# Gate and up products moved into the steps of attention, down and output projection into one last stage

## The reference

```
xn = layernorm(x)
# attention: 32 query heads, 8 key/value heads of width 32, causal, rotary positions
q, k, v = rope(xn @ wq), rope(xn @ wk), xn @ wv
s = softmax(mask(q @ k.T / sqrt(32))) @ v  @ wo
# feed-forward: 2,752 hidden features, weights packed in 4 bits with scales and zeros per group
W    = scale[group] * (nibble - (zero[group] + 1))
g    = silu( (silu(xn @ W_gate) * (xn @ W_up)) @ W_down )
out  = x + s * g
```

## Time and profile before

| | |
|---|---|
| median of three executions | 2513.79 us (2512.66 to 2514.32) |
| the profiled execution | 2516.59 us |
| its span, first to last instruction | 2514.5 us |
| mean granted clock of TensorE | 0.973 of 2.4 GHz |
| instructions | 46,178 |
| TensorE busy | 2377.0 us, 95% |
| VectorE busy | 1545.8 us, 61% |
| ScalarE busy | 748.2 us, 30% |
| GpSimd busy | 942.3 us, 37% |

### The profile page before, as it was taken

One profiled execution on the slowest core, in us unless ns is written; L12 is line 12 of the kernel. 1 busy time (PEld: TensorE's weight loads), 2 busy tenths in 40 slices (PEclk: granted clock), 3 DMA queues, 4 the chain that ended last, 5 costly groups with the idle time before them and its releaser, 6 DMA issues.

```text
span 2514.5 us, 46178 instructions
## 1 busy us (share of the span) xinstructions
PE 2377.0 (95%) x17048; PEld 1229.9 (49%) x17048; DVE 1545.8 (61%) x2800; ACT 748.2 (30%) x1469; POOL 942.3 (37%) x619
## 2 busy tenths in 40 slices
PE   6999889999999699989999999999999999999998
PEld 3555356666666444434444444444444444444432
DVE  4655488888888577355555555646454555556465
ACT  3222157777777532211111111010101010202022
POOL 2555469999999600021121212121212120202035
PEclk9999979999999899999999999999999999999998
DMA  5332312221222264200000000000000000000056
GB/s 159 97 84 64 86 43 72 72 71 59 70 72 72 89 198 163 82 16 13 12 13 13 12 12 12 5 19 3 21 0 24 0 24 0 24 0 19 0 172 234
DMA packets 129662, 138.26 MB, mean 55 GB/s; under 512 B 33106, under 2 KB 106421, under 8 KB 129148
## 3 DMA queue, kind: packets, MB, share of 16 engines
q1 hardware_dynamic: 127228, 127.96, 16.8%
q10 hardware_dynamic: 2304, 8.39, 0.8%
HBM read 88.76 MB, written 47.42 MB: 54 GB/s over the span
## 4 chain that ended last, share of the span: by engine, by line
PE 53%; DVE 3%; issue 1%; ACT 0%; POOL 0%; DVEq 0%; POOLq 0%
PE dn_ps L1474 18%; PE gate_ps L1455 17%; PE up_ps L1455 16%; PE s_ps L1424 1%; DVE zero L1542 1%; DVE wf L1554 0%; DVE dif L1548 0%; PE s_ps L1432 0%; ACT arena L1636 0%; PE z_ps L1424 0%; DVE acc L1586 0%; DVE nib L1523 0%; DVE zhalf L1537 0%; DVE idf L1502 0%; DVE acc L1579 0%
## 5 line engine op out<-in xcount | busy, mean ns | idle before, releaser
L1455 PE MATMUL gate_ps<-xT,wg 128*128 128x512 f16 x2112 | 789.1, 381 | 3.8 <-POOL wg L1676 3.8
L1455 PE MATMUL up_ps<-xT,wg 128*128 128x512 f16 x2016 | 766.1, 380 | 0.0
L577 POOL TENSOR_TENSOR p_lo<-probs 128x1152 f16<-128x1152 f32 (+1 forms) x256 | 501.2, 1994 | 48.8 <-ACT probs L741 48.7
L1474 PE MATMUL dn_ps<-wd,hT 128*128 128x512 f16 (+1 forms) x2112 | 471.9, 383 | 3.1 <-DVE acc L1579 3.1
L1676 POOL TENSOR_TENSOR wg<-wf,wg 128x512 f16<-128x512 f32 (+1 forms) x88 | 99.8, 1134 | 869.9 <-ACT wg L1622 869.9
L741 ACT ACTIVATE probs<-sc_ps 128x512 f32<-128x512 f32 (+3 forms) x768 | 351.0, 490 | 123.7 <-PE sc_ps L685 105.1
L1474 PEld LDWEIGHTS dn_ps<-wd,hT 128*128 128x128 f16 (+1 forms) x2112 | 202.2, 98 | 270.2 <-issue 31.5
L1579 DVE TENSOR_TENSOR acc<-acc,dn_ps 128x512 f32<-128x512 f32 x320 | 219.8, 687 | 184.7 <-PE dn_ps L1474 184.5
L1455 PEld LDWEIGHTS gate_ps<-xT,wg 128*128 128x128 f16 x2112 | 208.5, 99 | 242.0 <-issue 9.8
L790 DVE TENSOR_REDUCE shift<-mx_wide_ps 128x1 f16<-128x1024 f32 (+3 forms) x256 | 262.0, 1023 | 84.6 <-PE mx_wide_ps L667 84.5
L1455 PEld LDWEIGHTS up_ps<-xT,wg 128*128 128x128 f16 x2016 | 197.6, 98 | 229.9 <-issue 2.4
(11 more groups left out here) (130 smaller groups left out, 2973.7 us busy)
## 6 DMA issues: line engine op xcount, KB each, us to landing
o_scratch<-o SPq DMA_DIRECT2D x16, 1040.0 KB, 4.9
a<-o_scratch SPq DMA_DIRECT2D x16, 1040.0 KB, 5.4
arena<-q_scratch SPq DMA_DIRECT2D x48, 256.0 KB, 3.4
arena<-in_qw_d SPq DMA_DIRECT2D x42, 256.0 KB
xin<-in_x SPq DMA_DIRECT2D x16, 512.0 KB, 3.7
s_scratch<-arena ACTq DMA_DIRECT2D x16, 512.0 KB, 2.6
xT<-in_x SPq DMA_DIRECT2D x32, 256.0 KB, 4.8
xT<-s_scratch SPq DMA_DIRECT2D x32, 256.0 KB, 5.6
```

Of the source, the lines that this page charges most:

```text
L577: eng.tensor_tensor(p_lo[:, r % 2, c], probs[:, r % 2, c], p_hi[:, r % 2, c], ALU.subtract).then_inc(done, 1)
L1455: last = pe.matmul(to[q][:, :], wg[:, u, wp, s, g * P:(g + 1) * P], xT[:, xp, s, t * BANK:(t + 1) * BANK], start=(s == 0 and k == 0), stop ...
L1474: last = pe.matmul(dn_ps[n][:, :], hT[0:w, hp, e, tokens], wd[0:w, wp, e, n * BANK:(n + 1) * BANK], start=(e == 0 and p == 0), stop=(e == ...
```

## The change

`attend` and the gate and up part of `feed_forward` become one block, `attend_and_expand`. Its step is one head together with one unit, that is one tile of hidden features by one chunk of 512 tokens; there are 64 heads and 88 units, so 64 joint steps are followed by 24 with a unit alone, and ahead of them stand four lead-in steps with maxima and the first tile's weights. In each of the 8 slots of a step stand 6 gate or up products. Hidden values go to DRAM (`ht_d`), and so do the rebuilt down weights (`wd_d`).

Weights are rebuilt in half rounds of 256 columns, 12 to a tile. Zeros are no longer packed: their table is as wide as the scales' and is spread by a product with only the first 8 (down: 21) rows of the selection. VectorE doesn't unpack zeros any more.

Maxima use the high parts alone, 32 rows a head, and two heads go side by side: the loads place the high part of even heads in rows 0 to 31 and of odd heads in rows 32 to 63. The shifts are turned by VectorE. GpSimd forms all low parts of the probabilities.

The tables are built in `project_qkv`, 10 pieces over 20 of its blocks, and `xin` has 3 buffers there.

`finish` holds the output projection and the down projection: each tile of 128 tokens reads its hidden values from DRAM; down weights of all 22 tiles lie in the place of `xT` and elsewhere, and the sum over the 22 tiles stays in PSUM.

```diff
 def load_heads(eng, q_d, k_d, qT, kT, qk_loaded, g, u):
-    for piece, (qp, kp) in enumerate([(0, 0), (0, 1), (1, 0)]):
+    for piece, (qps, kp) in enumerate([((0, 1), 0), ((1, 0), 0), ((0,), 1)]):
...
# project_qkv
-    XB = 4
+    XB = 3
...
+            def tables_at(e):
+                c = (e - CT - 1) // 2
+                if 0 <= c < NP:
+                    piece(c, (e - CT - 1) % 2)
+                if e == CT + 2 * (NP + 1) + 2:
+                    select()
...
                 if e >= 1:
                     join(e - 1)
+                tables_at(e)
...
+def half_rounds(t):
+    halves = [(1, "g", 2 * t), (5, "g", 2 * t + 1)]
+    if t >= 2:
+        halves += [(3, "d", 2 * t - 4), (7, "d", 2 * t - 3)]
+    return sorted(halves)
...
# attend_and_expand
-    SC_BANKS = 3
+    SC_BANKS = 2
+    LEAD = 6
+    MAXIMA = [(7, 0), (7, 1), (0, 0), (6, 0), (6, 1), (1, 0), (5, 0), (2, 0), (5, 1), (4, 0), (3, 0), (4, 1)]
...
+            def maxima(m, r, k):
+                u, q, n = r // REP, r % REP, NM * pair(m, r) + k
+                t, c = MAXIMA[k]
...
+                if not isinstance(m, int) or n >= 1:
+                    pe.wait_ge(mx_taken, n)
+                first, end = c * BANK, min((c + 1) * BANK, (t + 1) * P)
+                diagonal = end == (t + 1) * P
+                for e in range(2):
+                    rows = slice(e * HD, (e + 1) * HD)
+                    last = pe.matmul(mx_ps[:, e, 0:end - first], qT[rows, u, q + e, t * P:(t + 1) * P],
+                                     kT[rows, u, first:end], start=True, stop=not diagonal)
+                if diagonal:
+                    for e in range(2):
+                        last = pe.matmul(mx_ps[:, e, t * P - first:end - first], identb[:, :], maskb[:, :],
+                                         start=False, stop=True)
+                last.then_inc(mx_ready, 1)
...
+            def rebuild(kind, n, j, u, number):
...
+                    rows = sel_gu[:, :].rearrange("g (p s) -> g s p", s=KT)[:, n, :]
+                    pe.matmul(sz_ps[:, 0, 0:2 * w], rows, st[:, u, :, 0:w], start=True, stop=True)
+                    last = pe.matmul(sz_ps[:, 1, 0:2 * w], rows[0:G_GU, :], zt[:, u, :, 0:w], start=True, stop=True)
+                else:
...
+                    pe.matmul(sz_ps[0:w, 0, :], sel[:, u, 0:w], scd[:, cols], start=True, stop=True)
+                    last = pe.matmul(sz_ps[0:w, 1, :], sel[0:G_D, u, 0:w], zd[:, cols], start=True, stop=True)
...
+            def step(m, r):              # TensorE
+                for i in range(ST):
+                    scores(m, r, i)
+                    for slot, kind, n, j, u, number, _ in halves(m, r):
+                        if slot == i:
+                            rebuild(kind, n, j, u, number)
+                    if maxima_at(m, r, i):
+                        maxima(*maxima_at(m, r, i))
+                    if i == 1:
+                        outputs(*at(m, r, -1, R), 0)
+                    if i >= 1:
+                        outputs(*at(m, r, -1, R), i)
+                    gate_up(m, r, i)
...
+            def step(m, r):              # ScalarE
+                for i in range(ST):
+                    exps(m, r, i)
+                    if i == 0:
+                        copy_sums(*at(m, r, -2, R))
+                    if i == 1:
+                        highs(*at(m, r, -1, R), 7)
+                    if i == 2:
+                        rounded(*at(m, r, -1, R))
+                    if i in (3, 5, 7):
+                        highs(m, r, i - 2)
+                    if i == 5:
+                        gated(m, r)
...
+            def step(m, r):              # VectorE
+                for i in range(ST):
+                    if i == 0:
+                        gated(*at(m, r, -1, R))
+                    if maxima_at(m, r, i):
+                        maxima(*maxima_at(m, r, i))
+                    for slot, kind, n, j, u, number, p in halves(m, r):
+                        if slot == i:
+                            rebuild(kind, n, j, u, number, p)
+                    if i == 2:
+                        select(m, r)
...
+            def step(m, r):              # GpSimd
+                low(m, r, 0)
+                lows(*at(m, r, -1, R), 7)
+                hidden(*at(m, r, -1, R))
+                low(m, r, 1)
+                lows(m, r, 1)
+                low(m, r, 2)
+                lows(m, r, 3)
+                low(m, r, 3)
+                lows(m, r, 5)
...
+            def step(m, r):              # SyncE
+                if r % 2:
+                    send_shift(*at(m, r, 1, R))
+                store_hidden(*at(m, r, -1, R))
+                store_down(*at(m, r, -1, R))
+                refill_values(*at(m, r, -2, R))
+                store_sums(*at(m, r, -3, R))
+                refill_weights(m, r)
+                prefetch(m, r)
+                refill_heads(m, r)
...
# finish, TensorE; n is a tile of 128 tokens
+            def tile(m, u):
+                n = number(m, u)
+                pe.wait_ge(ht_loaded[u], 32 * (m + 1))
+                for half in range(2):
+                    pe.wait_ge(g_done, 2 * (n - 2) + half + 1)
+                    for j in range(FTILES):
+                        down(u, half, j)
...
+            def body(m):
+                for u in range(2):
+                    turn(m + 1, u)
+                    tile(m, u)
+                    project(m + 1, u)
```

More of the change, by code:

```diff
@@ new lines, in unpack, with values @@
+            def unpack(words, g, to):
+                n = words.shape[1]
+                whole = tb_zn[0:g, 0:n * NIB].rearrange("g (c k) -> g c k", k=NIB)
+                def values():
+                    for k in range(NIB):
+                        last = dve.tensor_scalar(whole[:, :, k], words, 4 * k, 15,
+                                                 ALU.logical_shift_right, ALU.bitwise_and)
+                    return last
+                return [values, lambda: dve.tensor_copy(to, tb_zn[0:g, 0:n * NIB])]
@@ new lines, in finish, with wd_of, number, exists @@
+        wd_loaded = [sem(f"wd_loaded{i}") for i in range(len(groups))]
+        x_v = x.rearrange("b (t p) d -> (b t) p d", p=P)
+        out_v = out.rearrange("b (t p) d -> (b t) p d", p=P)
+        def wd_of(j):
+            for i, (to, at_tile, first, n) in enumerate(groups):
+                if first <= j < first + n:
+                    return i, to[:, :, at_tile + j - first, :]
+        def number(m, u):
+            return 2 * m + u
+        def exists(m, u):
+            return inside(m, u, TT)
@@ L994, in step, with gate @@
-            def step(m, u):
-                high(*at(m, u, 2))
-                turned(*at(m, u, 1))
-                post(m, u)
+                    act.wait_ge(out_stored[u], 16 * m)
+                act.activation(s_out[:, u, :], out_ps[:, :], ACT.Copy, scale=1.0 / W_SCALE).then_inc(s_done, 1)
+            def gate(m, u, half):
+                n = number(m, u)
+                act.wait_ge(dn_ready, 2 * n + half + 1)
+                if not isinstance(m, int) or n >= 1:
+                    act.wait_ge(prod_done, 2 * (n - 1) + half + 1)
+                act.activation(g[:, half, :], dn_ps[u][:, half, :], ACT.Silu, scale=1.0 / (W_SCALE * H_SCALE)
+                               ).then_inc(g_done, 1)
@@ L1010, in _, with body @@
             turned(1, 0)
-            post(0, 0)
-            post(0, 1)
-            with act.Fori(1, TT // 2 - 1) as m:
-                step(m, 0)
-                step(m, 1)
-            step(TT // 2 - 1, 0)
-            step(TT // 2 - 1, 1)
+            for u in range(2):
+                for half in range(2):
+                    gate(0, u, half)
+            take(1, 0)
+            turned(1, 1)
+            take(1, 1)
+            high(2, 0)
+            high(2, 1)
+            def body(m):
+                for u in range(2):
+                    turned(m + 1, u)
+                    gate(m, u, 0)
+                    gate(m, u, 1)
+                    take(m + 1, u)
+                    high(m + 2, u)
@@ L1019, in _ @@
+            bodies(act, body)
         @block.vector
@@ L1134, in _ @@
+            normalise(0, 0)
+            low(0, 0)
+            normalise(0, 1)
+            low(0, 1)
+            turned(0, 0)
+            normalise(1, 0)
+            low(1, 0)
+            turned(0, 1)
+            normalise(1, 1)
+            low(1, 1)
+            turned(1, 0)
+            for u in range(2):
+                for half in range(2):
+                    weigh(0, u, half)
+            turned(1, 1)
             for u in range(2):
-                normalise(1, u)
-                low(1, u)
@@ L1137, in _, with body @@
-            turned(1, 0)
-            with dve.Fori(1, PIECES // 2 + 1) as m:
+                normalise(2, u)
+                low(2, u)
+            def body(m):
                 for u in range(2):
-                    step(m, u)
-                    piece(m - 1, u)
```

(28 more changed lines are left out.)

1483 lines of the change are left out of this document (670 added, 813 removed).

## The result

The changed kernel takes 2608.8 us (four runs, 2605.2 to 2610.0) against 2513.8 for the kernel before on the same chip: a ratio of 1.0376, 95% interval 1.0358 to 1.0394. The change makes the kernel 95 us slower. The forecast was 2530, with 2600 as its upper bound.

The account below looks back on a forecast made before the run. TensorE, busy 95% of the span, was taken as the bound, so only its idle time could be won by overlap. Terms: 306 + 57 + 1,198 + 36 + 256 + 19 + 649 + 9 = 2,530 us; range 2,420 to 2,600.

Parts of the forecast that it names:

- the term for the tables in the q/k/v stage: q/k/v stage: ten table pieces over 20 blocks hidden except at two chunk borders; 4 us (0 to 15), stage 306.
- The core: Joint steps: TensorE's products, table products and shape switches sum to 18.9 us per step, 1,198 us for 64 steps.
- ScalarE's term: Joint steps: table loads delay slot 6's exponential, so slot 7's second score product waits; 0.35 us per step, 22 us.
- the loop pauses: Joint steps: five pauses at the first score product, one for each repeat of the loop body; 14 us.
- Two maxima side by side: Joint steps: two heads' 32-row maxima run at once, so 1.96 us per head falls to 1.14 with weight loads.
- Rival D: Joint steps: the two maxima don't overlap; 52 us more, 2,582; chance 0.12.
- The switch of array shape: TensorE in joint steps: each narrow-product excursion costs 0.20 us in and out; 1.6 us per step.
- Rival B: TensorE: shape switches cost little with 32 rows or less; 110 us less, 2,420; chance 0.13.
- Rival F: ScalarE in joint steps: a table switch costs twice the trace's row; 64 x 2.6 us more, 2,696; chance 0.04.
- Rival E: Joint steps: another engine's queue sets the slots; 1 us more per step, 2,594; chance 0.11.
- Rival C: Seams and queues are cheaper: lead-in 20, ScalarE 22, loops 14 us less; 2,474; chance 0.13.
- the lead-in: Seam before joint steps: 15 us of block end and loads, 32 of double maxima, 10 of half rounds; 57 us.

Follow-up runs that it names:

- with the operations spread: Changed kernel, table pieces split between VectorE and ScalarE, each operation one block behind the one it needs, scale selection ahead of all pieces: 2569.4 us, ratio 1.0231.
- one-product run: Changed kernel with scales and zeros side by side in one tile, so one 512-column product replaces the scales' and the zeros' product: 2579.8 us, ratio 1.0259.
- two-engine run: Changed kernel with ScalarE making the tables' three type-changing copies and two moved copies, VectorE keeping the rest behind statistics and turned copy: 2598.4 us, ratio 1.0338.

## Why the prediction was wrong

**The step that failed is the term for the tables in the q/k/v stage**, "4 us (0 to 15): 306". It measured 59. Two things in it were wrong.
- The price. A piece was taken at 5.9 us from the earlier trace rows, which lie in a stage where GpSimd is idle. With the tables VectorE is busy 92 us more (256.6 - 164.3), 4 of them the selection: 8.8 for each of ten pieces. The q/k/v stage was the one in which GpSimd was busy 139 of 302 us, and that number stood in the same table as VectorE's 164. With short GpSimd instructions the pieces took 5.0 each: the size was read rightly and holds for another stage.
- The cover. "Hidden" was read from an average, and a tight one: by the prediction's own sum 6.4 us in blocks of 6.6. With 8.8 a piece the same average is 7.9, over the block by 1.3 us, some 26 us in 20 blocks; that accounts for under half of the 59. The work comes in blocks of 5.2 us of TensorE with all of a block's statistics, rotation and table piece in one queue, and when a piece doesn't fit, the next rotation is late, then the turned x, then TensorE, whose granted clock was lower too in this stage. The 193 us of VectorE's time in the run with short GpSimd instructions were hidden in place (302.6 us); 213, with the operations spread, were not, by 19 us; 257 were not, by 59. Whether pieces of 5.0 us among the other long instructions would have been hidden, no run shows: they would make 218 us.

The terms of the joint part, one by one:
- The core, 18.9 us per step, with 36 for ScalarE and loop repeats, gives 19.3 (1,234 for the stretch). It measured 19.42 and 1,246. Right as to mechanism, 12 us too small: 7 of them are ScalarE's term (below), the loop pauses were 12.3 for 14, and the rest is 1,205 for 1,198.
- Two maxima side by side: they do run at once. Two products of 512 columns take 0.39 us together and two of 128 0.23, and the mask product after the first starts 0.31 later:

```profile
1459.86 0.39 PE L968 MATMUL mx_ps<-arena 32*128 32x512 f16 x2
1460.17 0.29 PE L972 MATMUL mx_ps<-maskb,identb 128*128 128x128 bf16 x2
...
1462.10 0.23 PE L968 MATMUL mx_ps<-arena 32*128 32x128 f16 x2
```

  Rival D is out.
- The switch of array shape: 0.25 us per excursion to 8 rows by the one-product run, 0.20 forecast. For 32 rows the starts have 0.31 us from a full product of 512 columns to the maxima and 0.32 from the maxima to the next, where 0.216 is the slot: 0.20 in and out. A down rebuild next to maxima did merge with them, as forecast. Rival B, which needed less than 0.16, is out.
- ScalarE: two loads of 1.28 us in most steps, as forecast. "0.35 us per step, 22 us" was too small: taking them away gave 34 us, 28 of them in the steps (64 x 0.44), and 48 with the one product (2579.8 - 2531.5). The forecast's mechanism, a late exponential and a bank not free for the second score product of slot 7, is what the runs bear out, at that very product, 0.45 us late in each of the 64 steps. Rival F (twice the row's price) is out, as the step was 19.4 us.
- Rival E, another engine's queue at +1 us per step: not in the joint part. In the q/k/v stage it is what happened, and there I had no rival for it.
- Rival C: the lead-in was 62 us, not cheaper than 57: 22 before its first product (15 forecast), 40 for the rest (42 forecast). The loop pauses were 12.3, near.
- 24 units alone 259.5 for 256; the second seam 19.2 for 19; the last stage 654 for 649. At the end of the second seam TensorE waits 11.6 us for ScalarE, in the last stage 2.1 for ScalarE and 7.9 for VectorE at the start, and never for the 14 MB from DRAM. The tail was 5.5 us for 9.

With the measured 59 for 4, and nothing else mended, the sum would have been 2,585, inside the range; the other 22 us are many small terms, nearly all of one sign.

Left open: how the 59 us divide between the pieces' waits behind GpSimd, the work itself and the rotation's own waits. Not tried: the rotation's instructions with GpSimd's waits and the table pieces without them.

## What to carry to other kernels

A duration belongs to the stage it was read in: before an instruction of VectorE is moved, look what GpSimd does in the stage where it will run, and if it is busy, price the instruction at its own time plus the rest of a GpSimd instruction, unless the trace shows its kind running beside GpSimd at its own time. Cover is to be counted block by block in the in-order queue, with the queue's waits, not as a busy share of the stage: here 44 us less of VectorE's busy time gave back 40 us with the operations spread, and 37 less gave back 11 where its queue waited for ScalarE. And a function of ScalarE that alternates with another table's is worth rewriting in the table that is loaded: the engine was 55% busy in the steps, and its table loads still cost 34 us, and 48 with TensorE's part shortened. A wait can be longer than its idle time, since the product before it covers its start: compare starts.

## What the runs showed of the hardware

- VectorE instructions of some kinds, started beside a running GpSimd instruction, end 0.37 to 0.73 us after it (the first of the shifts on 8 partitions 0.09 us), and their waiting is shown as busy time: 507 became 1970 ns. It was seen for a scaling and a change of type from float32 to bfloat16, for shifts on 8 partitions (348 against 230 ns) and for operations with two inputs in SBUF (872 ns, or 2.23 us). Operations with an input in PSUM, and the statistics of x, kept their time (0.69 against 0.67 us, 0.68 against 0.67).
- ScalarE's copies of 688 columns took 759 to 777 ns on the mean in the two-engine run, on 8, 32 or 72 partitions alike, with GpSimd busy 141 of 350 us: no such wait is seen in them.
- An excursion of TensorE to 8 rows and back cost 0.25 us for products of 256 columns, one to 32 rows 0.20 us; two 32-row products of 512 columns ran in the time of one (0.39 us), and a 32-row product started 7 ns after one of 21 rows.
- A table load is 1283 ns in every one of the 131 cases.
